# Second attention: the row sums of two units moved ahead of the copies on VectorE, the inversion behind the maxima

## The reference, cut to what matters

```python
q = (ln @ Wq).reshape(b, m, h, d).transpose(0, 2, 1, 3)
kv = jnp.concatenate([xn @ Wkv, ln @ Wkv], axis=1)
...
qn = rmsnorm(q, qn_g) * scale
kn = rmsnorm(k, kn_g)
sim = jnp.einsum('bhid,bhjd->bhij', qn, kn)
...
sim = jnp.where(padded_mask[:, None, None, :], sim, max_neg)
attn = jax.nn.softmax(sim.astype(jnp.float32), axis=-1).astype(sim.dtype)
out = jnp.einsum('bhij,bhjd->bhid', attn, v)
out = out.transpose(0, 2, 1, 3).reshape(b, m, h * d)
return out @ Wout + bout
```

## Time and profile before

| | us |
|---|---|
| median of 3 runs | 2242.23 (2241.12 to 2246.44) |
| the profiled execution | 2242.01 |
| its span in the trace | 2240.2 |
| TensorE matmul busy | 1945.1 (87%) |
| VectorE busy | 1274.5 (57%) |
| ScalarE busy | 1017.9 (45%) |
| GpSimd busy | 605.9 (27%) |

### The profile page before, as it was taken

The page is one execution under the profiler, slowest core; times in us unless marked ns, Lnnn a source line. Parts: engine busy times, 40 slices in busy tenths (PEclk is TensorE's granted clock), DMA queues, the critical chain, the costliest instruction groups (busy, mean ns, idle before and its releaser), DMA issues. The chain is left out here.

```text
span 2240.2 us, 40112 instructions
## 1 busy us (share of the span) xinstructions
PE 1945.1 (87%) x13656; PEld 1669.3 (75%) x13657; DVE 1274.5 (57%) x2963; ACT 1017.9 (45%) x1747; POOL 605.9 (27%) x555
## 2 busy tenths in 40 slices
PE   4888948999479999998999999999999994799994
PEld 2568948999367777777877877777778774699994
DVE  4273065676756666766676666667766776122223
ACT  2543315554245455544554555455545551344441
POOL 2300012333251432343143314323432300122220
PEclk9998958999689999999999999999999995899997
DMA  5502162111322211211321122122212207311113
GB/s 193 168 35 94 38 246 94 47 49 42 112 56 67 60 31 45 67 41 28 67 67 38 30 67 55 32 50 67 51 30 56 60 1 266 120 38 34 36 37 125
DMA packets 93663, 159.24 MB, mean 71 GB/s; under 512 B 22385, under 2 KB 54831, under 8 KB 91707
## 3 DMA queue, kind: packets, MB, share of 16 engines
q1 hardware_dynamic: 82875, 134.32, 21.3%
q0 software_dynamic: 8320, 20.65, 3.1%
q10 hardware_dynamic: 2304, 2.10, 0.3%
HBM read 71.57 MB, written 32.41 MB: 46 GB/s over the span
## 5 line engine op out<-in xcount | busy, mean ns | idle before, releaser
L1823 ACT ACTIVATE a_prob<-a_slot,a_npeak 128x1024 f32<-128x1024 f32 x256 | 285.7, 1116 | 307.1 <-DVE a_npeak L1882 306.8
L1880 DVE TENSOR_REDUCE a_part_peak<-a_slot 128x1 f32<-128x512 f32 (+1 forms) x512 | 349.2, 724 | 13.3 <-PE a_slot L1689 13.3
L1689 PE MATMUL a_slot<-a_KHL,a_QHL 128*128 128x512 f32 (+1 forms) x1536 | 317.5, 356 | 1.7 <-ACT a_latT L1257 1.7
L1689 PEld LDWEIGHTS a_slot<-a_KHL,a_QHL 128*128 128x128 f32 x1536 | 260.2, 189 | 47.6 <-ACT a_latT L1257 2.1
L1639 PE MATMUL a_side<-a_W,a_latT 128*128 128x128 f32 x1536 | 217.5, 294 | 80.3 <-DVE a_KT L1890 62.8
L1639 PEld LDWEIGHTS a_side<-a_W,a_latT 128*128 128x128 f32 x1536 | 192.9, 202 | 114.5 <-DVE a_KT L1890 77.2
L1714 PE MATMUL a_po<-a_probT,a_V 128*64 128x256 f32 (+1 forms) x2304 | 276.8, 385 | 0.0
L1698 PE MATMUL a_slot<-ident,a_prob 128*128 128x128 f32 x2048 | 276.6, 280 | 0.0
L1835 ACT ACTIVATE a_probT<-a_slot 128x640 f32<-128x640 f32 x256 | 180.5, 705 | 197.6 <-PE a_slot L1698 196.2
L1698 PEld LDWEIGHTS a_slot<-ident,a_prob 128*128 128x128 f32 x2048 | 244.4, 146 | 9.2 <-issue 1.2
L1903 DVE COPY a_probT<-a_slot 128x512 f32<-128x512 f32 x256 | 176.9, 691 | 90.8 <-PE a_slot L1698 89.3
(11 more groups left out here) (319 smaller groups left out, 2984.4 us busy)
## 6 DMA issues: line engine op xcount, KB each, us to landing
a_KHL<-a_KT SPq DMA_DIRECT2D x128, 256.0 KB, 4.1
a_QHL<-a_QT SPq DMA_DIRECT2D x128, 128.0 KB, 2.4
m_up<-_L_ffn_gate_up_proj_dram SPq DMA_DIRECT2D x8, 1024.0 KB, 9.7
m_up<-in_L_ffn_W_dram SPq DMA_DIRECT2D x8, 1024.0 KB, 9.0
m_down<-in_L_ffn_W_dram SPq DMA_DIRECT2D x8, 1024.0 KB, 13.2
a_prob_dram<-a0p_zeros SPq DMA_DIRECT2D x4, 1632.0 KB
a_dist_dram<-a_dist SPq DMA_DIRECT2D x4, 1632.0 KB, 8.2
a_band_prob<-a_prob_dram SPq DMA_DIRECT2D x4, 1632.0 KB, 6.8
```

Of the source, the lines that this page charges most:

```text
L1689: ins = t_.matmul(out[:, lo:hi], q, KHL[:, pair.parity, h, part, lo:hi], start=part == 0, stop=part == 1)
L1823: a_.activation(prob[:, u % 2, 0:SEQ], slot[u % 2][:, 0:SEQ], ACT.Exp, bias=bias, accum_out=latent_sum[:, u % 2:u % 2 + 1])
L1880: v.tensor_reduce(part[:, i:i + 1], slot[u % 2][:, lo:hi], AX.X, ALU.max).then_inc(part_peaked, 1)
```

## The change

VectorE's part of a step is written in another order. Nothing is added to it or left out. `row_sum(pair, u)` is now the first thing in a step, ahead of `normalise`; `row_sum(pair, u + 1)` stands behind `normalise` and ahead of `copy_sums` and of both copies. `invert` goes behind the two maxima. The other engines' programs are the same, row for row.

```diff
                 for u in range(0, UNITS, 2):
                     one_before, two_before = group_before(pair, u, 1), group_before(pair, u, 2)
+                    row_sum(pair, u)
                     if u % 4 == 0 and two_before[0]:
                         normalise(*two_before)
+                    row_sum(pair, u + 1)
                     if u % 4 == 2 and one_before[0]:
                         dve.wait_ge(turned, (pair.g * UNITS + u) * 3 + 1)
                         copy_sums(*one_before)
@@
                     copy_first(pair, u + 1)
-                    row_sum(pair, u)
-                    row_sum(pair, u + 1)
-                    if u % 4 == 2:
-                        invert(pair, u // 4)
                     for k in range(2):
                         nxt = ahead(pair, u + k, 2)
                         if nxt[0]:
                             peak(*nxt)
+                    if u % 4 == 2:
+                        invert(pair, u // 4)
                     if after and u in BOUND_AT:
                         bound(after, BOUND_AT.index(u))
```

## The result

The changed kernel takes 2147.68 us (median of 4 runs, 2146.72 to 2150.84), the kernel before 2242.35: a ratio of 0.9577 with a 95% interval of 0.9561 to 0.9594. The forecast was 2155 us, 87 us less; it became 95 us less.

A forecast was written before the change was run, and what follows sets the result against it. TensorE's waits, above all for VectorE's key piece in u=6, and half clock behind them were taken as the bound: 64.5 + 22.4 + 1.0 + 0.5 - 1.2 = 87.2 us off 2242.0 gives 2155 us, range 2145 to 2170.

The forecast's parts named there:

- TensorE's waits: Second attention: TensorE gets back 4.3 us a pair of its waits for VectorE and ScalarE, 64.5 us over 15 pairs.
- the bound of 4.86 us a pair: Second attention: all of TensorE's listed waits, 72.9 us over 15 pairs, the most it can get back.
- u=6: Step u=6: maxima right behind the copies let TensorE go on at 1212.65 instead of 1215.72, 3.1 us a pair.
- u=8, 10 and 12: Steps u=8, 10 and 12: earlier maxima give TensorE 0.45, 0.27 and 0.5 us, together 1.2 us a pair.
- Half clock: TensorE behind the 3.4 us waits: half clock goes with them, 21 us for 14 pairs and 1.4 for the first, 22.4.
- rival A: Pairs: the clock does not come back, from another cause or because a shorter wait suffices; 2177 us, chance 9%.
- Row sums in front: Row sums ahead of the copies, under VectorE's wait for TensorE's turning: cost nothing, at most 15 us if cover is thinner.
- my slack: Step u=12: 0.88 us between the first copy's end and the scores, said to cover a copy 0.15 us late.
- What I expected of the profile: Profile after: row sum's mean falls from about 0.45 us, none exceeds 2.2 us, key piece wait under 12 us, clock 1.00.
- The power: Steps u=6 and u=10: row sums run beside GpSimd's raising to a power, 3.23 us, and are not held.
- Rival B: Steps u=6 and u=10: GpSimd's power holds VectorE's row sums, scores start about 2.1 us late; 2249 us, chance 5%.
- Ends: First pair gains 1.0 us in u=2, last pair 0.5; four loop turns lose 1.2 us to row sums ahead of `normalise`.

The follow-up runs named there:

- The late key piece of the experiments: Changed kernel with five or two spare-tile maxima on VectorE ahead of the key piece of u=6: 2229.75 us with five, 2172.11 us with two.

## Why the prediction was right, step by step

*TensorE's waits.* They were the right thing to count, and the bound of 4.86 us a pair was nearly reached: 4.76 instead of the 4.3 forecast. The mis-sized term is u=6, forecast at 3.1 and measured at about 3.5 (step 12.0 to 8.5 us), because I gave the widening 1.0 us behind folds of GpSimd. It took 0.29 and at most 0.39 there: it got in between two folds. That was close: in all 15 pairs it began only 0.03 to 0.3 us ahead of the next fold (0.86 us long in the pair shown), and a hold by that fold is what I had allowed for. u=8, 10 and 12 gave 0.34, 0.36 and 0.60, together 1.3 for 1.2. Over 15 pairs this term is 71 us instead of 64.5.

*Half clock.* 22.4 us forecast; measured are 19.4 in the middle pairs and about 1.5 in the first. Eight of the 11 falls in the kernel before cost 1.4 to 1.7 us each; the other three lasted twice as long and cost 2.6 to 2.8. The late key piece of the experiments confirms the cause, and rival A falls. My sentence that waits of about 0.5 us are never followed by it holds; from about 2 us on it may follow or not.

*Row sums in front.* Costed at nothing, and this was right for the changed kernel, in which u=4 and u=14 are not longer than before. But my slack was thin: the doubled row sums broke through it in just the two steps that I had named. What I expected of the profile failed here. The mean row sum did not fall from 0.454 us; it rose, and the longest took 2.23 us instead of at most 2.2:

```profile
L1912 DVE CUSTOM_DVE_ANT_0 a_masked<-a_prob,a_maskf,a_latent_sum 128x77 f32<-128x77 f32 x256 | 124.6, 487 | 117.4 <-ACT a_prob L1824 100.2 <-issue 16.9
```

The holds did not go; they moved under a wait for TensorE. In u=4 both row sums are held and the copy still waits for the turning:

```profile
722.17 2.23 DVE L1912 CUSTOM_DVE_ANT_0 a_masked<-a_prob,a_maskf,a_latent_sum 128x77 f32<-128x77 f32 x1
722.20 2.11 POOL L1580 TENSOR_TENSOR a_square<-a_knat 128x1152 f32<-128x1152 f32 x1 [24.31 <-ACT a_V L1808]
...
724.66 1.22 DVE L1912 CUSTOM_DVE_ANT_0 a_masked<-a_prob,a_maskf,a_latent_sum 128x77 f32<-128x77 f32 x1
...
726.18 0.69 DVE L1903 COPY a_probT<-a_slot 128x512 f32<-128x512 f32 x1 [0.29 <-PE a_slot L1698]
```

*The power.* Sixty row sums of the changed kernel lie beside a power on GpSimd, 48 of them wholly inside it, and took 0.29 to 0.30 us each. One of them:

```profile
1159.41 3.25 POOL L1570 TENSOR_TENSOR a_kinv<-a_kvar,a_expo 128x18 f32<-128x18 f32 x1 [3.39 <-DVE a_kvar L1897]
...
1161.80 0.30 DVE L1912 CUSTOM_DVE_ANT_0 a_masked<-a_prob,a_maskf,a_latent_sum 128x77 f32<-128x77 f32 x1 [2.21 <-ACT a_prob L1824]
```

Rival B falls. The Trainium skill (SBUF — State Buffer, "Who interferes with whom") lets a GpSimd instruction that reads SBUF hold a VectorE one with two SBUF inputs for its whole length; that fits the squaring (row sums of 2.23 us beside it), the folds and the splitting (1.22 us) here, and does not fit the power.

*Ends.* First pair: 6.9 us, of which 4.3 + 1.4 + 1.0 = 6.7 had been forecast. Last pair: 2.3 us instead of 0.5; I had called it bound by TensorE, but six of its first seven steps went from 7.2 to 7.5 us down to 6.92 to 7.04. The loop turns cost 2.1 us instead of 1.2, most of it at the one behind which the clock fell, which I had not counted. The sum was 87 us for a measured 94 to 95; the 7 us come from u=6 and the last pair.

## What to carry to other kernels

Work that nobody waits for soon belongs where its engine waits anyway, and whether it fits is read from the slack behind that wait, with the time included for which another engine can hold it. Bound the gain by the idle time of the engine that sets the pace, and look at what the idle time does to its clock: here a wait behind which the clock fell cost 1.4 to 1.7 us more than it lasted, in three cases 2.6 to 2.8. A hold by another engine is an event, not a property of the place: count in how many rounds it occurs before its price enters a sum.

## What the runs showed of the hardware that was not expected

- Half clock follows some waits of TensorE and not others of the same length, oftener the longer ones (none of 15 at 1.2 us, 7 of 15 at about 2, 15 of 15 at 3.2 to 3.4, 11 of 15 at 3.4 to 3.7).
- GpSimd's power over 128x18 elements lasts 3.25 us and holds no row sum (0.29 to 0.30 us each), while its product over 128x1024 elements holds one for the whole of 1.9 us.
- A turn of the hardware loop costs 2.0 to 2.5 us, and 3.7 where the clock falls behind it; TensorE and VectorE then stand still without a releaser for up to 2.0 and 4.0 us. The middle pairs written out, three times as much code, showed no such stall.
